# Attention of a mixer kernel: the row maxima's way into the query stack, and the order of VectorE's routing work

## The reference

```python
q = jnp.einsum('btd,hdk->bhtk', x, Wq)
k = jnp.einsum('btd,hdk->bhtk', x, Wk)
v = jnp.einsum('btd,hdk->bhtk', x, Wv)
scores = jnp.einsum('bhqk,bhsk->bhqs', q, k) * scale
scores = jnp.where(causal, scores, -jnp.inf)
weights = jax.nn.softmax(scores, axis=-1)
out = jnp.einsum('bhqs,bhsk->bhqk', weights, v)
out = out @ Wo.T + bo
```

```python
logits = jnp.einsum('btd,de->bte', x, gate_w)
probs = jax.nn.softmax(logits, axis=-1)
expert_weights, expert_indices = jax.lax.top_k(probs, TOP_K)
```

## Time and profile before

| | us |
|---|---|
| three runs | 959.59, 961.8, 966.61 |
| median of the runs | 961.8 |
| profiled execution, first to last instruction (span) | 956.6 |
| PE busy | 656.8 |
| VectorE busy | 581.4 |
| GpSimd busy | 355.4 |
| ScalarE busy | 344.0 |

### The profile page before, as it was taken

One profiled execution on the slowest core, in us unless ns is written; L12 is line 12 of the kernel. 1 busy time (PEld: TensorE's weight loads), 2 busy tenths in 40 slices (PEclk: granted clock), 3 DMA queues, 4 the chain that ended last, 5 costly groups with the idle time before them and its releaser, 6 DMA issues. The chain is left out here.

```text
span 956.6 us, 19471 instructions
## 1 busy us (share of the span) xinstructions
PE 656.8 (69%) x6492; PEld 449.0 (47%) x6492; DVE 581.4 (61%) x1765; ACT 344.0 (36%) x597; POOL 355.4 (37%) x674
## 2 busy tenths in 40 slices
PE   2688784788784214999722799688677982398990
PEld 0354453444464204999711244344343442398990
DVE  7978843878733762666550776665556743366763
ACT  2223242344344302444223066354353561143430
POOL 0323321233542473777637001203302222376771
PEclk9799998899996556999955599898988995699995
DMA  9201399211200013555427400600600000254544
GB/s 219 88 23 46 95 214 141 66 46 46 81 4 1 31 53 86 157 151 155 122 88 189 104 3 3 147 3 22 149 3 13 15 16 12 69 157 138 160 141 140
DMA packets 100274, 81.20 MB, mean 85 GB/s; under 512 B 7708, under 2 KB 92124, under 8 KB 99436
## 3 DMA queue, kind: packets, MB, share of 16 engines
q1 hardware_dynamic: 95632, 70.58, 29.7%
q0 software_dynamic: 4544, 9.38, 2.9%
HBM read 54.76 MB, written 23.40 MB: 82 GB/s over the span
## 5 line engine op out<-in xcount | busy, mean ns | idle before, releaser
L1246 DVE TENSOR_REDUCE rmax<-PA 128x1 f32<-128x512 f32 (+3 forms) x256 | 120.6, 489 | 104.8 <-PE PA L1930 98.2
L774 POOL DMA_INDIRECT outs_dram<-va,ids x78 | 95.0, 1218 | 57.0 <-POOL ids L770 27.3
L759 POOL DMA_INDIRECT rows_dram<-va,idx x64 | 63.8, 998 | 129.1 <-DVE va L1129 111.2
L1887 PE MATMUL PC<-ffn_w,pm 128*128 128x128 f32 x624 | 87.7, 283 | 12.5 <-DMA ffn_w<-in_w 12.1
L1930 PE MATMUL PA<-kst,qst 96*128 96x512 bf16 (+3 forms) x256 | 85.1, 338 | 0.0
L1887 PEld LDWEIGHTS PC<-ffn_w,pm 128*128 128x128 f32 x624 | 75.7, 191 | 16.4 <-DMA ffn_w<-in_w 15.5
L1657 PE MATMUL P<-const,xn 128*128 128x128 f32 x92 | 18.7, 340 | 92.6 <-ACT xn L1448 31.9
L1928 PE MATMUL PA<-mqb,idb 128*128 128x128 bf16 x256 | 61.0, 239 | 29.6 <-DMA qst<-qst 14.5
L1176 DVE SCALAR_TENSOR_TENSOR pm<-PB,invb,decay 128x512 f32<-128x512 f32 x78 | 58.1, 744 | 38.3 <-ACT decay L1513 38.1
L1505 ACT ACTIVATE kv_b<-P 128x256 f16<-128x256 f16 x78 | 30.0, 384 | 133.8 <-PE P L1866 133.8
L1600 ACT ACTIVATE pm<-PB 128x1024 f32<-128x1024 f32 (+1 forms) x64 | 45.0, 703 | 81.0 <-PE PB L1953 80.9
(11 more groups left out here) (241 smaller groups left out, 1496.1 us busy)
## 6 DMA issues: line engine op xcount, KB each, us to landing
ffn_w<-in_w SPq DMA_DIRECT2D x78, 256.0 KB, 2.9
rows_dram<-wall SPq DMA_DIRECT2D x1, 8385.0 KB, 46.3
X<-in_w SPq DMA_DIRECT2D x32, 256.0 KB, 2.9
proj_w<-rows_dram SPq DMA_DIRECT2D x78, 65.0 KB
qst<-parts_dram SPq DMA_DIRECT2D x12, 384.0 KB
kst<-parts_dram SPq DMA_DIRECT2D x12, 384.0 KB
parts_dram<-qkp SPq DMA_DIRECT2D x16, 256.0 KB, 2.5
X<-in_x SPq DMA_DIRECT2D x8, 256.0 KB, 4.6
```

Of the source, the lines that this page charges most:

```text
L759: nc.gpsimd.indirect_dma_start(out=rows_dram, out_offset=bass.IndirectOffsetOnAxis(ap=idx[:, t, r:r + 1], axis=0), in_=xrow[:, t, :], in_o ...
L774: nc.gpsimd.indirect_dma_start(out=outs_dram, out_offset=bass.IndirectOffsetOnAxis(ap=ids[:, k % YB:k % YB + 1], axis=0), in_=ysb[:, k % Y ...
L1246: nc.vector.tensor_reduce(rmax[:, i, h % HG:h % HG + 1], PA[:, n % 2, 0:(i + 1) * P], AX_X, ALU.max).then_inc(pair_sb[n % 2], 1)
L1887: ins = mm(PC[:, k % 2, 0:D], eT[:, k % 2, f, :], w2b[k % WB2][:, f, :], start=f == 0, stop=f == FB - 1)
```

## The change

1. Sync's maxima and the DRAM tensor go. ScalarE, right after its copy to mxT, waits for that copy and issues one DMA from mxT to the three rows of qst. Its next copy to mxT waits for that DMA (max_in) where it waited for the first hop (max_out).
2. Sync issues the stacks of all four sequences one after the other, with the waits they had.
3. add_out keeps the addition at unit 7; the sums (out_sums) come at unit 8 and the means at unit 9, and ScalarE's normalization at unit 13 instead of 12.
4. The plan has mt, rt and ct at units 15, 17 and 24 instead of 14, 16 and 22; ScalarE's exponentials of the logits come at unit 21 instead of 20.
5. In attention route runs in four pieces on units 18 to 21, and choose_slots in three on units 25, 26 and 27. The instructions and their order are those of before; only row maxima come between.

```diff
-        out += {3: [("tr", s - 1, 1)], 5: [("ao", s - 1)], 7: [("wo", s - 1)], 14: [("mt", s - 1)],
-                16: [("rt", s - 1)], 22: [("ct", s - 1)]}.get(v, [])
+        out += {3: [("tr", s - 1, 1)], 5: [("ao", s - 1)], 7: [("wo", s - 1)], 15: [("mt", s - 1)],
+                17: [("rt", s - 1)], 24: [("ct", s - 1)]}.get(v, [])
...
-            def maxima(g):
-                b = (g // NG) % 2
-                o = (g % NG) * HG * L
-                wait_pair(sp, "mx", g)
-                if g >= 1:
-                    sp.wait_ge(max_in, 16 * g)
-                sp.dma_start(max_dram, mxT).then_inc(max_out, 16)
-                sp.wait_ge(max_out, 16 * (g + 1))
-                sp.dma_start(qst[KQ:KQ + NP3, b, o:o + HG * L], max_dram.rearrange("(i h) n -> i (h n)", h=HG)
-                             ).then_inc(max_in, 16)
...
-            stacks(0)
-            stacks(1)
-            for g in range(NG * SEQ):
-                maxima(g)
-                if g % NG == 0 and 1 <= g // NG < SEQ - 1:
-                    stacks(g // NG + 1)
+            for s in range(SEQ):
+                stacks(s)
...
-                        if v == 18 and s >= 1:
-                            route(1, s - 1)
-                        if v == 25 and s >= 1:
-                            choose_slots(1, s - 1)
+                        if s >= 1:
+                            if v == 8:
+                                out_sums(s - 1)
+                            if v == 9:
+                                mean_variance((LAYERS + 1) * SEQ + s - 1)
+                            if v == 18:
+                                less_largest(1, s - 1)
+                                compare(1, 0)
+                            if v == 19:
+                                compare(1, 1)
+                                compare(1, 2)
+                            if v == 20:
+                                compare(1, 3)
+                                earlier_first(1)
+                            if v == 21:
+                                ranks(1, s - 1)
+                            if v == 25:
+                                pick_shares(1, s - 1)
+                            if v == 26:
+                                pick_slots(1, s - 1)
+                            if v == 27:
+                                low_rows(1, s - 1)
...
                             if s >= 1:
-                                act.wait_ge(max_out, 16 * s)
+                                act.wait_ge(max_in, 16 * s)
                             ins = nc.scalar.activation(mxT, src[0:NP3 * HG, :], ACT.Copy)
...
+                        if what == "mx":
+                            maxima(s)
+
+                def maxima(g):
+
+                    b = (g // NG) % 2
+                    o = (g % NG) * HG * L
+                    wait_pair(act, "mx", g)
+                    act.dma_start(qst[KQ:KQ + NP3, b, o:o + HG * L], mxT).then_inc(max_in, 16)
...
-                        if v == HV - 4 and s >= 1:
+                        if v == HV - 3 and s >= 1:
                             normalize(LNM2, s - 1)
                             high_rows(1, s - 1)
-                        if v == 20 and s >= 1:
+                        if v == 21 and s >= 1:
                             exp_logits(1, s - 1)
```

More of the change, by code:

```diff
@@ L364, in mixer_kernel @@
         amax_dram = nc.dram_tensor("amax_dram", (P, E), F32, kind="Internal").ap()
-        max_dram = nc.dram_tensor("max_dram", (NP3 * HG, L), BF16, kind="Internal").ap()
         PA = ps("PA", [P, 2, 512])
@@ L411, in mixer_kernel @@
         st_in = (sem("st_ina"), sem("st_inb"))
-        max_out = sem("max_out")
         max_in = sem("max_in")
@@ L1072, in route, with less_largest @@
             def route(m, s):
+                less_largest(m, s)
+                for k in range(TPS):
+                    compare(m, k)
+                earlier_first(m)
+                ranks(m, s)
+            def less_largest(m, s):
                 c = m * SEQ + s
-                cgt, cge = cgt_[m], cge_[m]
                 wait_router(dve, m, s)
@@ L1081, in route, with compare, earlier_first, ranks @@
                                         ALU.subtract).then_inc(lg_d, 1)
[L1082 to L1085, removed]
+            def compare(m, k):
+                for o, op in ((cgt_[m], ALU.is_gt), (cge_[m], ALU.is_ge)):
+                    ins = nc.vector.tensor_tensor(o[:, k, :, :], bc(lg[:, k, :], [P, E, E], 1),
+                                                  bc(lg[:, k, :], [P, E, E], 2), op)
                 link(ins)
-                flat = cge.rearrange("p k a b -> p k (a b)")
+            def earlier_first(m):
+                flat = cge_[m].rearrange("p k a b -> p k (a b)")
                 link(nc.vector.tensor_tensor(flat, flat, bc(const[:, C_TRI:C_TRI + E * E], [P, TPS, E * E], 1),
                                              ALU.mult))
+            def ranks(m, s):
+                c = m * SEQ + s
+                cgt, cge = cgt_[m], cge_[m]
                 link(nc.vector.tensor_tensor(cgt, cgt, cge, ALU.max))
@@ L1097, in choose_slots, with pick_shares @@
             def choose_slots(m, s):
+                pick_shares(m, s)
+                pick_slots(m, s)
+                low_rows(m, s)
+            def pick_shares(m, s):
                 c = m * SEQ + s
@@ L1101, in choose_slots @@
                 rk = rank[:, c % 2, :, :]
-                slot, hit = slot_[m], hit_[m]
+                hit = hit_[m]
                 flat = lambda ap: ap.rearrange("p k e -> p (k e)")
@@ L1115, in choose_slots, with pick_slots @@
                 nc.vector.tensor_tensor(w12[:, r, 1], w12[:, r, 0], e2[:, 0, :], ALU.mult)
+            def pick_slots(m, s):
+                c = m * SEQ + s
+                r = slice(TPS * s, TPS * s + TPS)
+                rk = rank[:, c % 2, :, :]
+                slot, hit = slot_[m], hit_[m]
+                flat = lambda ap: ap.rearrange("p k e -> p (k e)")
                 wait_count(dve, m, s)
@@ L1127, in choose_slots, with low_rows @@
                 nc.vector.tensor_copy(xrow[:, r, D:D + 1], sl[:, 1, :].unsqueeze(2))
+            def low_rows(m, s):
+                c = m * SEQ + s
+                r = slice(TPS * s, TPS * s + TPS)
                 dve.wait_ge(hi_sb, c + 1)
@@ L1284, in add_out, with out_sums @@
                                             X[:, r, :], ALU.add).then_inc(pair_sb[n % 2], 1)
+                def out_sums(s):
                     wait_pair(dve, "wo", s)
@@ L1311, in attention @@
                             spread_values(s + 1, 0)
-                        if v == 18 and s >= 1:
-                            route(1, s - 1)
-                        if v == 25 and s >= 1:
-                            choose_slots(1, s - 1)
+                        if s >= 1:
[20 more added lines that the diff above has]
+                                low_rows(1, s - 1)
                 run(LAST_USES)
+                out_sums(SEQ - 1)
+                mean_variance((LAYERS + 1) * SEQ + SEQ - 1)
                 dve.wait_ge(av_ps, NV * SEQ)
```

1 line of the change is left out of this document (removed).

## The result

The changed kernel takes 948.4 us (median of 4 runs, 945.4 to 950.7); the kernel before, run again beside it, takes 964.2 us (4 runs, 959.6 to 966.7). The ratio is 0.985 (95% interval 0.982 to 0.988): faster by about 1.5%. The forecast was 940.6 us with a range of 931 to 952.

What follows compares the result with a forecast made beforehand. TensorE was taken to set the pace in attention, pausing for the maxima's transfer and VectorE's blocks. Gains of 25.7 less losses of 4.5, net 21.2 us, took 961.8 to 940.6 us, range 931 to 952.

Steps and rivals of the forecast that it cites:

- Step 1: Maxima's transfer for unit 8 of sequences 1 and 2: gains 17.6 us of waits, 1.0 clock, 1.0 spread sums.
- Step 2: ScalarE's sixteen waits and issues of the copy: 0.35 us each, hidden except at two places, 0.7 us lost.
- Step 3: Routing in four pieces, units 16 to 23 of sequences 1 and 2: 17.53 to 15.3 us, gain 4.4 us.
- Step 4: Choice of slots in three pieces, sequence 2's last group: 14.58 to 12.9 us, gain 1.7 us.
- Step 5: End of sequence 1: later slots delay GpSimd's scatter, residual and exponentials, 2.6 us lost, plus 1.2 us by slower clock.
- Step 6: Last sequence: counts and slots two units later, GpSimd's scatter ends 793.6 instead of 791.2 us, hidden with 1.4 us cover.
- the held transfer: Rival: the copy waits until the stack loads drain, saving only the second hop, 1.7 us twice; 955.8 us; chance 0.11.
- held in its issue: Rival: the copy's issue holds ScalarE until the loads drain, PE waits 22.3 us; 963.9 us, slower; chance 0.04.
- the chain through GpSimd: Rival: with the last slots piece earlier, the end of sequence 1 gains instead of losing; about 935 us; chance 0.12.

Runs made afterwards that it cites:

- experiment 4: Changed kernel with Sync holding the stack loads until the maxima of the previous sequence's second group have landed: 936.4 us, ratio 0.974 to the kernel before.
- experiment 5: Changed kernel with each of the six loads of a stack cut in four along the row, 4 KB pieces for 16 KB: 935.6 us, ratio 0.973.
- experiment 3: Changed kernel with the single copy issued by Sync, in its old order between the stacks, instead of by ScalarE: 951.7 us, ratio 0.990.
- experiments 1: Changed kernel with VectorE's routing, slots and sums back in single pieces at their old units, only the new transfer kept: 949.1 us, ratio 0.988.
- experiment 6: Changed kernel with GpSimd's residual of sequence 3 moved ahead of the scatter of sequence 0's rows: 935.0 us, ratio 0.971.
- experiment 7: Changed kernel with both the stack loads held until the maxima land and GpSimd's residual ahead of the scatter: 930.5 us, ratio 0.967.
- experiment 8: Experiment 7 with GpSimd's second subtraction of the residual cut into four pieces: 933.3 us, ratio 0.968 to the kernel before.

## Why the prediction was right, and where its sum was off

The forecast, faster by over 1%, was right, and 948.4 us lies in the range, 7.8 us above the likeliest value. Against attention's groups:

| step | forecast, us | measured, us |
|---|---|---|
| 1, transfer, clock and sums (groups 0 and 1 of sequences 1 to 3) | +19.6 | +12.5 |
| 2, ScalarE's issues | -0.7 | -1.1 |
| 3, routing groups | +4.4 | +5.9 |
| 4, choice of slots, sequence 2 | +1.7 | +2.1 |
| 5, last group of sequence 1; clock behind it | -2.6; -1.2 | -2.5; -1.5 |
| elsewhere (sequence 0, last group) | 0 | -0.8 |
| sum | 21.2 | 14.6 |

The measured column is made of differences of the groups above; step 5's clock is units 0 to 6 of sequence 2, 10.92 us before and 12.46 after, and is taken out of step 1. Step 1 fell 7.1 us short; steps 3 and 4, 1.9 us better than forecast, hid part of that.

**Step 1 was mis-sized, and it is the miss.** I took "the lower side, since what delayed the store was order within one queue", and wrote that up to about 10 us it is hidden. The order within the queue was only the smaller part of the delay: from the issue until PE goes on it fell from 17.2 and 16.5 us to 12.5 and 14.5 (the copies land after 11.5 and 13.5), where a copy by itself lands after 1.6. What is left comes from going beside the loads on another queue: with the loads held back (experiment 4) the same copies land in 1.6 us. The landings are beyond 10 us, so 7.2 us of waiting are left, with the slow clock behind them. That the term was otherwise right in sum is shown by experiment 5: with the copies landing in 3.3 and 3.5 us, groups 0 and 1 of sequences 1 to 3 give back 19.7 us, the clock's loss of step 5 in it, where my steps came to 19.6 - 1.2 = 18.4. Its smallest part was too small: sequence 3, which has no transfer wait, gained 1.7 us in these groups (27.62 to 25.91), where I put 0.35 for the spread sums and 1.16 at most.

I weighed two rules of the Trainium skill (DMA: Bandwidth & Descriptors). The section "Queues, rings and completion order", by which an engine goes round the queues packet by packet, agrees with the trace: rounds of small packets 1.3 us apart among large ones of 1.25 us. A packet of that section is a bundle of descriptors, and no run shows whether the profile's packets are the same thing. By turns of one profile packet it doesn't give the 7.2 us until the first packet, 5.8 more than a copy alone needs. "Issuing engines are not separate DMA queues", by which spreading saves little more than issue time, understates it here: the issuer alone, one hop by Sync against one by ScalarE, is 15.5 against 7.2 us of waiting. Of that, 3.8 us are the earlier issue, and 3.8 and 0.7 us are the copies' own way in sequences 1 and 2, where one issue takes 0.7.

**Step 2.** The issue took 0.73 us, not 0.35, and is hidden nearly everywhere as I wrote. I took the price from Sync's issues to and from DRAM. The copy at the end of the stacks, which like the new one stays within SBUF, stood in the trace of before, right ahead of the store of the earlier trace rows, and took twice that, so that "0.4 us at most" around the loads was misread:

```profile
604.34 0.70 SPq L555 DMA_DIRECT2D qst<-qst  x1
```

Where PE waits for ScalarE's copy of the weighted sums in sequence 3, the group lost 1.1 us; with Sync as issuer (experiment 3) it lost 0.1. With the issue on ScalarE, experiments 1, 6 and 7 lost 2.5 to 2.7 us there, because the granted clock fell behind the wait (0.85 on the group's mean); in the changed kernel it stayed at 1.00.

**Step 3.** Laid out by hand: four waits of 0.3, 0.75, 0.25 and 1.1 us. In the trace (order of time, sequence 1) the router bank's is 0.20, and unit 19's, 21's and 23's:

```profile
643.19 0.65 PE L2027 MATMUL PA<-const,decay 128*128 128x128 f32 x4 [0.69 <-DVE rmax L1264]
...
645.94 0.23 PE L1976 MATMUL PA<-mqb,idb 128*128 128x128 bf16 x1 [0.32 <-DVE rmax L1264]
...
648.98 0.23 PE L1976 MATMUL PA<-mqb,idb 128*128 128x128 bf16 x1 [0.85 <-DVE rmax L1264]
```

The groups are 14.6 us against 15.3, and the granted clock is 1.00 from 636 to 660 us, as forecast. **Step 4** came out at 12.51 us against 12.9, by the same method.

**Step 5** was right in mechanism and size. GpSimd's and ScalarE's order, as in the earlier trace rows:

```profile
659.43 1.08 POOL L741 DMA_INDIRECT rows_dram<-va,idx  x1 [29.42 <-DVE va L1147]
...
669.37 2.13 POOL L654 TENSOR_TENSOR R<-qkf,qkp 128x1024 f32<-128x1024 f32 x1
```

```profile
671.53 1.06 ACT L1418 ACTIVATE qkp<-R 128x1024 bf16<-128x1024 f32 x1 [6.31 <-POOL R L654]
```

The scatter starts 6.7 us after unit 25 (652.73; I wrote some 7), and PE waits 5.44 us (I wrote about 5). Experiment 6 shows the cause: with the residual ahead of the scatter the wait is gone. **Step 6** held: behind attention GpSimd still waits for VectorE, 1.94 us where 3.83 were before and I expected 1.4.

Of the rivals, the held transfer is refuted (the copy is through at 620.34, when Sync's queue still has 28 packets to start); ScalarE was never held in its issue longer than 1.33 us; the chain through GpSimd was not covered.

## What to carry to other kernels

A small transfer put on another queue escapes the order of the first, but not the loads that it goes beside. Before calling it hidden, look when it is issued against them, read the time of one large packet off the queue's view, and count one per turn of the small transfer and some more ahead of its first (here about five). When a block is cut into pieces, the last piece sets when all that hangs on the block starts, so follow the other engines' orders behind it; moving one independent step ahead of that chain (experiment 6) shortened attention by another 9.0 us, where the whole change had given 14.6. A plain delay of the large loads until the small transfer is through (experiment 4) gave 9.1; both together gave 12.6, and the ratio to the kernel before went from 0.985 to 0.967.

## What the runs showed of the hardware

- A copy of 12 KB within SBUF took 1.6 us alone, 11.5 and 13.5 us beside loads in 16 KB packets, and 3.3 and 3.5 us beside loads of the same total in 4 KB packets, of which less stood ahead. What stood ahead of its first packet in the kernel after was, beyond the 1.4 us that it takes alone, some 4.6 and 5.6 large packets of 1.25 us; why that many stays open.
- The issue of this copy takes 0.73 us in the median on ScalarE and 0.70 on Sync (experiment 3), against 0.32 to 0.45 us for Sync's loads from DRAM beside it: the price goes with the transfer and not with the issuer.
- An instruction of VectorE on numbers in SBUF stood still, 1.81 us for 0.17, until GpSimd's subtraction under way had ended; row maxima, read from PSUM, ran beside GpSimd's subtraction at their usual 0.42 us (experiment 8, 661.19 us). The Trainium skill (SBUF — State Buffer, "Who interferes with whom") describes a shared pair of ports that the later engine gets only when the instruction holding it is over; experiment 8, where each hold ends at a boundary between pieces, agrees.
- TensorE's granted clock was 0.50 for 4.4 us behind a wait of 4.55 us, and 1.00 across the routing group with its waits of 0.85 us and less. Between these it went either way: 0.70 over the 4 us from the end of a wait of 2.09 us (experiment 7), 1.00 behind 1.89 us in the same place (experiment 8); behind the wait of 1.52 us in the third group of sequence 3 it stayed at 1.00 in the changed kernel and experiments 4, 5 and 8, and fell to 0.50 for 3.4 us in experiments 6 and 7.
